# Attention with four PSUM banks for the scores, q and its transposition in one bank, and two heads' transposed probabilities per copy

## The chip, the cores and the metric

The kernel runs on one core of one Trainium2 chip. The metric is the device time of one execution in microseconds, as the median of several runs. The same inputs and outputs hold for both versions. Eight PSUM banks of 512 fp32 elements per partition are available to a core; TensorE writes into them, VectorE and ScalarE read them.

## The reference, cut to what matters

A layer of attention (one key and value head for 16 query heads of 64, cosine scores with a relative position bias, a causal mask and a null key), a layer norm, and a feed-forward part with fake quantisation, added to x. x is (8, 256, 128).

```python
xn = ln(x, g_norm)
q = (xn @ Wq).reshape(b, n, HEADS, DIM_HEAD).transpose(0, 2, 1, 3)
kv = xn @ Wkv
k, v = (kv[..., :DIM_HEAD], kv[..., DIM_HEAD:])
...
q = l2norm(q) * q_scale
k = l2norm(k) * k_scale
sim = jnp.einsum('bhid,bjd->bhij', q, k) * SCALE
...
attn = jax.nn.softmax(sim, axis=-1)
out = jnp.einsum('bhij,bjd->bhid', attn, v)
out = out.transpose(0, 2, 1, 3).reshape(b, n, HEADS * DIM_HEAD)
return ln(out @ Wout, g_out)
...
x = x + ffn(attention(x))
```

## The kernel before, in words

Each engine has its own instruction stream, written out by hand; semaphores tie them together. The attention is a loop over groups (`over_groups`, L91): 8 batches of 4 groups of 4 heads, and two groups more to drain. The functions named `group` at L418 (GpSimd), L540 (ScalarE), L812 (TensorE) and L1172 (VectorE) each set their own engine's order. What belongs to one group of heads runs over three groups of the loop: scores and exponentials in its own, turning (transposing) the probabilities in the next (`turned`), the value product and the output product in the one after (`summed`).

For a pair of heads TensorE makes the scores (`scores`, L764) in banks 0 and 1, one head per bank, 258 columns for the second block of rows and 129 for the first. VectorE adds the bias and takes the row maximum (`score_pair`, L1113). ScalarE takes the exponential and the row sum (`exponent`, L516). VectorE inverts the row sums of a pair (`invert`), and GpSimd multiplies the probabilities by them (`normalise`, L410). TensorE turns each head's three 128-blocks (`turn`, L799) into bank 2 or 3, and ScalarE copies them into `pT`, 384 columns per head (`pT_evac`, L526). The value product (`values`, L783) goes into bank 4, VectorE copies it out (`oT_copy`), and `y_products` (L736) multiplies it by Wout into bank 7, over the four groups of a batch. `null_weights` (L730) and `y_null` add the null key's part.

In between, q of the next quarter batch (128 rows, 8 heads) is made: product (`q_make`, L638) into bank 5, square on ScalarE (`q_square`, L476), row sums on VectorE (`q_norm2`), power -0.5 on GpSimd (`q_power`, L380), scaling on VectorE (`q_normalise`, L981), transposition on TensorE (`qT_make`, L652) into bank 6, copy on VectorE (`qT_evac`, L988). Once per batch the same happens for x (normalised rows `xn`, `x_power` L372, transposed), for k and v (`kv_make`, `k_power`, `k_normalise` L971 which makes `kz`, `kT_make`), and for the layer norm of the output (`y_stats`, `y_power`, `y_normalise` L1138, `yT_make`). Their small transpositions share bank 6 with q's: at each group's end TensorE waits until VectorE has copied q out (`qT_ready`) and then makes the small one.

A score pair waits until VectorE has read the pair before it (`scored`), since both use banks 0 and 1:

```python
if g > 0:
    pe.wait_ge(scored, 2 * g)
```

Of the kernel before, what the change touches and what calls it, by code (L numbers as in the profile page):

```python
# [33 lines left out]
P = 128  # L34
# [24 lines left out]
class Group:  # L59


    def __init__(self, at):
        self.at = at
        self.b, self.g = at // GB, at % GB
        self.par = self.b % 2
# [8 lines left out]
        self.made = c + 1 if 4 <= c + 1 < GB * B else None  # L74

# [21 lines left out]
def build(nc, x, cond, mask, g_norm, Wq, Wkv, q_scale, k_scale, null_bias, w0, b0, g0, w1, b1, g1, w2, b2,  # L97
# [3 lines left out]
    with ExitStack() as ctx:  # L101
# [122 lines left out]
        bank = [ctx.enter_context(nc.psum_tensor(f"bank{i}", [P, 512], F32)) for i in range(8)]  # L224
        score_ps, trans_ps = bank[0:2], bank[2:4]
        val_ps, q_ps, qT_ps, misc = bank[4], bank[5], bank[6], bank[7]
# [4 lines left out]

        null_out = qT_ps[0:H, N:2 * N]
# [119 lines left out]
        def _(pool):  # L352
# [55 lines left out]
            q_power(3, 3)  # L408

# [8 lines left out]
            def group(s):  # L418
                if s.quarter is not None and s.quarter >= 4:
                    q_power(s.quarter, s.quarter % 4)  # L420
                if s.g == 2 and s.prev is not None:
                    y_power(s.prev)
                if 1 <= s.at < GB * B:
                    normalise(heads(s.at - 1)[2:4])
                if s.at == GB * B:
                    normalise(heads(s.at - 1)[2:3])
                if s.g == 2 and s.next is not None:
                    k_power(s.next)
                if s.live:
                    normalise(heads(s.at)[0:2])  # L430
                if s.g == 1 and s.b + 2 < B:
                    x_power(s.b + 2)
# [17 lines left out]
        def _(act):  # L450
# [4 lines left out]
            def xT_evac(n, par, ps):  # L455
                act.wait_ge(xT_done, n + 1)
                act.copy(xTh[par][:, :], ps[:, 0:N]).then_inc(xT_ready, 1)
                act.copy(xTr[:, :], ps[:, 0:N][:, ::-1]).then_inc(xT_ready, 1)

            def kv_evac(n, ps):  # L460
                act.wait_ge(kv_done, n + 1)
                act.copy(kv[:, :, :], ps[:, 0:N].rearrange("p (t c) -> p t c", t=2)).then_inc(kv_ready, 1)

            def v_copy(n, par):
# [4 lines left out]
                act.copy(val[par][:, :, :], kv[:, :, D:2 * D]).then_inc(v_ready, 1)  # L469

            def kT_evac(n, par, ps):
                act.wait_ge(kT_done, n + 1)
                act.copy(kT[par][:, :].rearrange("p (b k) -> p b k", b=2)[:, :, 1:P + 1],
                         ps[:, 0:N].rearrange("p (b k) -> p b k", b=2)).then_inc(kT_ready, 1)
# [25 lines left out]
            kv_evac(0, misc)  # L500
# [8 lines left out]
            kT_evac(0, 0, misc)  # L509
            v_copy(0, 0)  # L510
# [833 lines left out]
```

## Time and profile before

| | |
|---|---|
| median of 3 runs | 310.94 us (310.54 to 310.96) |
| the profiled execution | 309.61 us |
| its span, first to last instruction | 307.8 us |
| mean granted TensorE clock | 0.975 of full |
| TensorE matmul busy | 262.3 us (85%) |
| TensorE weight loads busy | 207.9 us (68%) |
| VectorE busy | 242.8 us (79%) |
| ScalarE busy | 224.9 us (73%) |
| GpSimd busy | 206.6 us (67%) |

Busy times are of the whole span. The attention loop takes the span from 26 to 271 us; before it lie loads and the position table, behind it the feed-forward part. PE is TensorE, PEld its weight loads, DVE VectorE, ACT ScalarE, POOL GpSimd. A matmul's end in the profile is modelled: the next one of the same stream starts before it, so spacing is read from starts.

### The profile page before, as it was taken

The page shows a single profiled execution, that of the slowest core. Times are in us where ns is not written, and L with a number is a line of the kernel's source. Part 1 is how long each engine was busy: PE and PEld are TensorE (multiplying, and loading weights), DVE is VectorE, ACT ScalarE, POOL GpSimd, SP SyncE. Part 2 cuts the span into 40 slices and gives each one's busy share as a digit, 9 for nine tenths or more (in the row PEclk, how much of TensorE's full clock was granted, in tenths as well). Part 3 has the DMA queues.
Part 4 walks back from the last instruction along what each step waited for, and adds up shares of the span by engine and source line. Part 5 has one row for each costly group of instructions (what it writes and reads, how often), then busy time and mean ns, then how long its engine had stood idle before and what let it go on. Part 6 is the DMA issues. An engine that isn't in the chain of part 4 may idle for free.

```text
span 307.8 us, 7322 instructions
## 1 busy us (share of the span) xinstructions
PE 262.3 (85%) x2176; PEld 207.9 (68%) x2176; DVE 242.8 (79%) x976; ACT 224.9 (73%) x771; POOL 206.6 (67%) x393
## 2 busy tenths in 40 slices
PE   0767699999899989999998999899999998876251
PEld 0326578888688868877886888688878877561040
DVE  2978658788878888887888788868787876659985
ACT  1265678897889788978897888878888887437661
POOL 2786677679777877788789778887888755211401
PEclk9999699999999999999999999999999999999958
DMA  6369000000000000000000000000000020000005
GB/s 144 64 163 254 3 1 2 1 2 1 2 1 2 1 4 2 0 2 2 2 0 3 2 2 0 2 1 3 2 1 3 1 72 1 2 0 0 0 2 142
DMA packets 13084, 6.89 MB, mean 22 GB/s; under 512 B 1954, under 2 KB 12914, under 8 KB 13043
## 3 DMA queue, kind: packets, MB, share of 16 engines
q1 hardware_dynamic: 12466, 6.13, 8.0%
q8 instruction: 20, 0.33, 0.5%
q10 hardware_dynamic: 576, 0.26, 0.4%
q14 instruction: 22, 0.17, 0.2%
HBM read 5.31 MB, written 1.07 MB: 21 GB/s over the span
## 4 chain that ended last, share of the span: by engine, by line
PE 50%; DVE 21%; POOL 14%; issue 7%; ACT 5%; DMA 1%; ACTq 0%; POOLq 0%; DVEq 0%
PE bank L777 13%; PE bank L809 10%; PE bank L794 9%; PE bank L747 6%; POOL prob L415 5%; DVE score L1119 4%; PE bank L642 4%; POOL rq L370 3%; PE bank L658 3%; ACT prob L522 2%; DVE hmax L1252 2%; DVE kz L968 2%; DVE oT L1289 2%; DMA g0b<-in_L_cond_g_dram 1%; POOL rstd L370 1%
## 5 line engine op out<-in xcount | busy, mean ns | idle before, releaser
L522 ACT ACTIVATE prob<-score,negmax 128x258 f32<-128x258 f32 (+1 forms) x256 | 114.8, 454 | 30.3 <-DVE negmax L1119 30.1
L415 POOL TENSOR_SCALAR prob<-prob,rrow 128x258 f32<-128x258 f32 x254 | 109.2, 447 | 40.7 <-DVE rrow L1127 37.5
L1119 DVE CUSTOM_DVE_ANT_0 score<-bank,bias 128x258 f32<-128x258 f32 (+1 forms) x256 | 76.6, 355 | 20.9 <-PE bank L777 20.8
L532 ACT COPY pT<-bank 128x384 f32<-128x384 f32 x128 | 58.1, 480 | 15.3 <-PE bank L809 15.3
L777 PE MATMUL bank<-kT,qT 64*128 64x258 f32 (+1 forms) x512 | 60.1, 354 | 4.4 <-DVE negmax L1119 4.0
L777 PEld LDWEIGHTS bank<-kT,qT 64*128 64x128 f32 x512 | 44.6, 188 | 20.1 <-DVE negmax L1119 11.8
L809 PE MATMUL bank<-ident,prob 128*128 128x128 f32 x384 | 55.3, 280 | 1.0 <-ACT pT L532 1.0
L370 POOL TENSOR_TENSOR rq<-qn,neghalf 128x8 f32<-128x8 f32 x32 | 54.1, 1691 | 2.7
L809 PEld LDWEIGHTS bank<-ident,prob 128*128 128x128 f32 x384 | 43.7, 143 | 10.0 <-issue 1.7
L794 PE MATMUL bank<-pT,val 128*64 128x256 f32 (+1 forms) x512 | 48.7, 332 | 1.0 <-ACT pT L532 0.8
L522 ACT ACTIVATION_READ_ACCUMULATOR prob<-score,negmax 128x1 f32 x256 | 49.4, 193 | 0.0
L794 PEld LDWEIGHTS bank<-pT,val 128*64 128x64 f32 x512 | 31.7, 136 | 14.5 <-ACT pT L532 1.6
L747 PE MATMUL bank<-wout,oT 128*128 128x128 f32 x256 | 33.9, 275 | 0.8 <-DVE oT L1110 0.8
L747 PEld LDWEIGHTS bank<-wout,oT 128*128 128x128 f32 x256 | 31.1, 192 | 1.0 <-DVE oT L1110 1.0
L979 DVE TENSOR_REDUCE qn<-sq 128x8 f32<-128x512 f32 x32 | 21.6, 676 | 6.7 <-ACT sq L479 6.6
L1110 DVE COPY oT<-bank 128x512 f32<-128x512 f32 x32 | 21.8, 682 | 2.4 <-PE bank L794 2.4
L1127 DVE RECIPROCAL rrow<-rowsum 128x4 f32<-128x4 f32 x64 | 11.1, 174 | 14.5 <-ACT prob L522 14.5
L985 DVE TENSOR_TENSOR qn<-bank,rq 128x512 f32<-128x512 f32 x32 | 21.9, 685 | 0.6 <-POOL rq L370 0.3
L990 DVE COPY qT<-bank 128x512 f32<-128x512 f32 x32 | 21.5, 673 | 0.8 <-PE bank L658 0.8
L1119 DVE DVE_READ_ACCUMULATOR2_ANT negmax<- 128x1 f32 x256 | 21.2, 83 | 0.0
L658 PE MATMUL bank<-ident,qn 128*128 128x128 f32 x128 | 19.8, 278 | 0.7 <-DVE qn L985 0.7
L479 ACT ACTIVATE sq<-bank 128x512 f32<-128x512 f32 x32 | 18.8, 587 | 2.0 <-DVE qn L979 0.8
(161 smaller groups left out, 340.2 us busy)
## 6 DMA issues: line engine op xcount, KB each, us to landing
bias<-relative_table SPq DMA_DIRECT2D x8, 256.0 KB, 5.3
out_dram<-prob SPq DMA_DIRECT2D x4, 256.0 KB, 3.0
X<-in_x_dram SPq DMA_DIRECT2D x1, 896.0 KB, 12.1
prob<-in_L_cond_Wq_dram SPq DMA_DIRECT2D x1, 512.0 KB, 5.5
wout<-in_L_cond_Wout_dram SPq DMA_DIRECT2D x1, 512.0 KB, 13.3
prob<-in_L_ffn_w_down_dram SPq DMA_DIRECT2D x1, 176.0 KB, 2.4
X<-in_x_dram SPq DMA_DIRECT2D x1, 128.0 KB, 4.1
prob<-in_L_ffn_w_gate_dram SPq DMA_DIRECT2D x1, 128.0 KB, 2.0
```

Source lines behind the costliest of these rows:

```text
L370: pool.tensor_tensor(dst, src, neghalf[:, 0:width], ALU.pow).then_inc(done, 1)
L415: pool.tensor_scalar(prob[:, par, h, cols], prob[:, par, h, cols], rrow[:, par, h, t:t + 1], 1.0, ALU.mult, ALU.mult).then_inc(normed, 1)
L522: act.activation(prob[:, par, h, cols], score[:, h % 4, cols], ACT.Exp, scale=-1.0, bias=negmax[:, par, h, t:t + 1], accum_out=rowsum[:, p ...
L532: act.copy(pT[:, h % 4, :], trans_ps[h % 2][:, 0:3 * P]).then_inc(pT_ready, 1)
L658: last = pe.transpose(qT_ps[:, k * P:k * P + P], head_pair, ident[:, :])
L747: pe.matmul(y_out(t), oT[:, m % 2, k, t * P:t * P + P], wout[:, k, :], start=k + t == 0, stop=False, skip_group_check=True)
L777: product = pe.matmul(score_ps[a][:, at:at + KEYS1 - c0], qT[par][rows, h // 2, t * P:t * P + P], kT[par][rows, c0:KEYS1], start=not maske ...
L794: last = pe.matmul(val_ps[a * D:a * D + D, pair * N + i0:pair * N + N], val[m % 2][:, blk, :], pT[:, 2 * pair + a, c0:c1], start=blk == 1, ...
L809: last = pe.transpose(trans_ps[h % 2][:, k * P:k * P + P], prob[:, par, h, c0:c0 + P], ident[:, :])
L985: dve.tensor_tensor(qn[:, :, :], ps[:, :].rearrange("p (h d) -> p h d", d=D), rq[:, q, :].unsqueeze(2).broadcast_to([P, 8, D]), ALU.mult). ...
L1110: dve.tensor_copy(oT[:, m % 2, 2 * g:2 * g + 2, :].rearrange("p k n -> p (k n)"), val_ps[:, :])\
L1119: dve.tensor_tensor_reduce(score[:, h % 4, c0:c0 + w], ps[:, c0:c0 + w], bias[:, h, 0:w], -1.0, -3.0 * NEG, ALU.add, ALU.min, negmax[:, pa ...
```

## The change

PSUM is divided anew. `front` holds four score banks (0 to 3), two per pair of heads; `trans` (banks 4 and 5) receives the turned probabilities, and its second bank, bank 5, is also the value product's; q and its transposition share bank 6; bank 7 stays. The last 128 columns of both `trans` banks (`tails`) take the small transpositions and the null weights.

- `scores` uses the banks of its pair and waits for the scores of a whole group before. The value product comes first in a group, then both score pairs.
- `pT_evac` copies two heads, 768 columns, with one instruction; `values` waits for both copies.
- ScalarE's order is: q's square, exponentials of heads 2 and 3 of the group before, head 0, first copy, the small evacuation, head 1, second copy, null weights.
- TensorE interleaves the small transpositions with the first two turns; the next two turns wait for their evacuation (`low_out`). q's transposition stands between two halves of the output products, the q product at the group's end, behind q's copy.
- VectorE's and GpSimd's orders follow; yT is scaled by ScalarE, wql is made by GpSimd.

```diff
-        score_ps, trans_ps = bank[0:2], bank[2:4]
-        val_ps, q_ps, qT_ps, misc = bank[4], bank[5], bank[6], bank[7]
+        front = [psum(f"front{i}", 2) for i in range(2)]
+        trans = psum("trans", 2)
+        bank = [pair[:, i, :] for pair in (*front, trans) for i in range(2)]
+        bank += [psum(f"bank{i}", 1)[:, 0, :] for i in range(6, 8)]
+        score_ps, trans_ps = bank[0:4], bank[4:6]
+        val_ps, q_ps, misc = bank[5], bank[6], bank[7]
+        tails = trans[:, :, 3 * P:4 * P]
...
-            def pT_evac(at, i):
-
-                g, _, h = heads(at)[i]
-                act.wait_ge(pT_done, g + 1)
+            def pT_evac(at, pair):
+
+                g, _, h = heads(at)[2 * pair]
+                act.wait_ge(pT_done, g + 2)
                 if at > 0:
                     act.wait_ge(o_done, at)
-                act.copy(pT[:, h % 4, :], trans_ps[h % 2][:, 0:3 * P]).then_inc(pT_ready, 1)
+                ps = front[pair] if at == GB * B - 1 else trans
+                act.copy(pT[:, 2 * pair:2 * pair + 2, :], ps[:, :, 0:3 * P]).then_inc(pT_ready, 1)
...
+                if s.quarter is not None and s.quarter >= 4:
+                    q_square(s.quarter, q_ps)
+                if s.turned is not None:
+                    exponent(heads(s.turned)[2])
+                    exponent(heads(s.turned)[3])
                 if s.live:
                     exponent(heads(s.at)[0])
...
+                if s.turned is not None:
+                    pT_evac(s.turned, 0)
...
-                if g > 0:
-                    pe.wait_ge(scored, 2 * g)
+                banks = score_ps[2 * pair:2 * pair + 2]
+                if g >= GH:
+                    pe.wait_ge(scored, 2 * (g - 2))
...
-                pe.wait_ge(pT_ready, GH * (at + 1))
+                pe.wait_ge(pT_ready, 2 * (at + 1))
...
+                elif g > 1 and g % 2 == 0:
+                    pe.wait_ge(pT_ready, g // 2)
+                if i == 1 and s.summed is not None:
+                    pe.wait_ge(oT_ready, s.summed + 1)
+                if i < 2:
+                    low_make(s, i)
+                if i == 2:
+                    low_out(s)
+                if i >= 2 and s.null is not None and not last:
+                    if i == 2:
+                        pe.wait_ge(normed, 2 * g + 4)
+                    null_weights(s.null, i - 2)
...
+                if s.summed is not None:
+                    if s.g == 1 and s.prev is not None:
+                        pe.wait_ge(n_ready, s.prev + 1)
+                    values(s.summed)
...
                 if s.made is not None:
+                    pe.wait_ge(qT_ready, s.made)
```

How the order moves is seen at two places.

TensorE around a value product, in the loop's early groups, before (banks 0 and 1 scores, 2 and 3 turns, 4 values, 7 output):

```order
L747 MATMUL bank7<-wout,oT 128x128 [waits oT_ready]
L747 MATMUL bank7<-wout,oT 128x128 x3
L754 MATMUL bank7<-unull,pnT 128x128 [waits n_ready]
L754 MATMUL bank7<-unull,pnT 128x128
L628 MATMUL bank6<-wkv,xTr 128x128 [waits xT_ready,qT_ready]
L628 MATMUL bank6<-wkv,xTr 128x128
L777 MATMUL bank0<-kT1,qT1 128x258 [waits scored,qT_ready]
L777 MATMUL bank1<-kT1,qT1 128x258
L777 MATMUL bank0<-kT1,qT1 128x129
L777 MATMUL bank1<-kT1,qT1 128x129
L794 MATMUL bank4<-pT,val1 64x256 [waits oT_ready,v_ready,pT_ready]
L794 MATMUL bank4<-pT,val1 64x256
```

The same engine now, from q's transposition to the next value product:

```order
L696 MATMUL bank6<-ident,qn 128x128 [waits qT_ready,q_norm]
L696 MATMUL bank6<-ident,qn 128x128 x3
L792 MATMUL bank7<-wout,oT 128x128 x2
L888 MATMUL trans<-ident,prob 128x128 [waits xT_ready,pT_ready,normed]
L888 MATMUL trans<-ident,prob 128x128 x2
L888 MATMUL trans<-ident,prob 128x128 [waits normed]
L888 MATMUL trans<-ident,prob 128x128 x2
L680 MATMUL bank6<-wqh,xTh0 128x512 [waits q_norm,qT_ready]
L680 MATMUL bank6<-wql,xTh0 128x512
L680 MATMUL bank6<-wqh,xTl0 128x512
L835 MATMUL trans<-pT,val1 64x256 [waits oT_ready,pT_ready]
L835 MATMUL trans<-pT,val1 64x256
```

Before, the output products, the small ones and a score pair stood between the last turn and the value product; now it is the q product alone, and the value product writes the bank that was turned into.

VectorE in a batch's third group, before (from the row sums of k squared; yn is the normalised output, oT the copied value product):

```order
L962 ISA ksq,kn2<-kv 128x64 [waits kv_ready]
L962 ISA kn2 128x1
L962 ISA ksq,kn2<-kv 128x64
L962 ISA kn2 128x1
L985 TENSOR_TENSOR qn<-bank5,rq 128x512 [waits qT_done,q_rq]
L1142 TENSOR_SCALAR yn<-bank7,omv,ors 128x128 [waits y_rstd]
L1142 TENSOR_SCALAR yn<-bank7,omv,ors 128x128
L1110 COPY oT<-bank4 128x512 [waits o_done]
L1119 ISA score,negmax<-bank0,bias 128x258 [waits s_done]
L1119 ISA negmax 128x1
L1119 ISA score,negmax<-bank0,bias 128x129
```

And now:

```order
L1202 TENSOR_SCALAR yn<-bank7,omv,ors 128x128 [waits y_rstd]
L1202 TENSOR_SCALAR yn<-bank7,omv,ors 128x128
L1179 ISA score,negmax<-front0,bias 128x258 [waits s_done]
L1179 ISA negmax 128x1
L1179 ISA score,negmax<-front0,bias 128x129
L1179 ISA negmax 128x1
L1179 ISA score,negmax<-front0,bias 128x258 [waits s_done]
L1179 ISA negmax 128x1
L1179 ISA score,negmax<-front0,bias 128x129
L1179 ISA negmax 128x1
L1046 TENSOR_TENSOR qn<-bank6,rq 128x512 [waits qT_done,q_rq]
```

The scaling of q (`qn<-bank,rq`) stood behind both heads of a pair and right ahead of yn; now yn is ahead of the first scores, and they ahead of q's scaling.

## Rows read from the trace of the kernel before

**Rows 1.** Windows: us, each engine's busy us (xcount), PEclk, DMA share, GB/s

```profile
33.05:39.90 6.85, 5.38 (x23) 4.58 (x24) 5.08 (x26) 3.79 (x15) 4.04 (x9) 0.50 0.00 0
...
117.40:147.40 30.00, 28.92 (x256) 23.88 (x252) 24.61 (x109) 24.75 (x90) 24.12 (x47) 1.00 0.01 2
...
207.30:236.20 28.90, 28.89 (x256) 23.89 (x254) 23.79 (x105) 24.65 (x90) 23.09 (x45) 1.00 0.01 3
236.20:256.10 19.90, 19.42 (x175) 15.64 (x173) 14.88 (x72) 16.40 (x62) 14.24 (x31) 1.00 0.10 28
```

**Rows 2.** Order of time, TensorE, one batch: start us, us, what [idle before]

```profile
139.26 0.44 PE L635 MATMUL bank<-ident,kz 128*128 128x128 f32 x2 [1.08 <-DVE qT L990]
...
140.48 1.52 PE L794 MATMUL bank<-pT,val 128*64 128x256 f32 x16
142.00 0.93 PE L777 MATMUL bank<-kT,qT 64*128 64x258 f32 x8
142.86 0.88 PE L809 MATMUL bank<-ident,prob 128*128 128x128 f32 x6
...
143.93 0.47 PE L642 MATMUL bank<-wqh,xTh 128*128 128x512 f32 x1
...
144.70 0.82 PE L809 MATMUL bank<-ident,prob 128*128 128x128 f32 x6
145.35 1.06 PE L747 MATMUL bank<-wout,oT 128*128 128x128 f32 x8
```

**Rows 3.** Order of time, ScalarE, the same stretch

```profile
141.21 0.51 ACT L522 ACTIVATE prob<-score,negmax 128x258 f32<-128x258 f32 x1 [1.10 <-DVE negmax L1119]
...
142.10 0.50 ACT L522 ACTIVATE prob<-score,negmax 128x258 f32<-128x258 f32 x1
...
143.44 0.86 ACT L532 COPY pT<-bank 128x384 f32<-128x384 f32 x2 [0.37 <-PE bank L809]
```

**Rows 4.** Lines by form: busy us, mean ns, idle before; ScalarE's copies out of PSUM

```profile
L532 ACT COPY pT<-bank 128x384 f32<-128x384 f32 x128 | 58.1, 480 | 15.3 <-PE bank L809 15.3
...
L462 ACT COPY kv<-bank 128x256 f32<-128x256 f32 x8 | 3.0, 374 | 3.1 <-PE bank L628 2.8
```

**Rows 5.** Order of time, the last groups: a copy and the value product behind it

```profile
262.38 0.47 ACT L532 COPY pT<-bank 128x384 f32<-128x384 f32 x1
...
262.90 1.52 PE L794 MATMUL bank<-pT,val 128*64 128x256 f32 x16 [0.77 <-ACT pT L532]
```

**Rows 6.** Order of time, VectorE

```profile
126.33 0.68 DVE L985 TENSOR_TENSOR qn<-bank,rq 128x512 f32<-128x512 f32 x1
...
127.53 0.41 DVE L1119 CUSTOM_DVE_ANT_0 score<-bank,bias 128x258 f32<-128x258 f32 x1
...
128.64 0.17 DVE L1127 RECIPROCAL rrow<-rowsum 128x4 f32<-128x4 f32 x1
...
140.74 0.43 DVE L1119 CUSTOM_DVE_ANT_0 score<-bank,bias 128x258 f32<-128x258 f32 x1 [0.86 <-PE bank L777]
```

**Rows 7.** Lines by form: VectorE's products for kz

```profile
L968 DVE SCALAR_TENSOR_TENSOR kz<-kv,rk,qks 128x128 f32<-128x128 f32 x16 | 6.0, 414 | 1.7 <-POOL rk L370 1.7
```

**Rows 8.** Order of time, GpSimd

```profile
131.81 0.25 POOL L368 TENSOR_SCALAR qn<-qn 128x8 f32<-128x8 f32 x1
...
133.89 0.19 POOL L366 TENSOR_SCALAR omv<-omv 128x2 f32<-128x2 f32 x1
...
134.96 1.66 POOL L415 TENSOR_SCALAR prob<-prob,rrow 128x258 f32<-128x258 f32 x4
136.70 0.23 POOL L368 TENSOR_SCALAR kn<-kn 128x2 f32<-128x2 f32 x1
```

**Rows 9.** Start: GpSimd's first normalisation, its widest product, group four's value product

```profile
30.97 4.48 POOL L415 TENSOR_SCALAR prob<-prob,rrow 128x258 f32<-128x258 f32 x8 [2.44 <-DVE rrow L1127]
...
L443 POOL TENSOR_TENSOR prob<-prob 128x512 f32<-128x512 f32 x4 | 5.1, 1268 | 12.3 <-ACT prob L608 12.3
...
57.38 1.52 PE L794 MATMUL bank<-pT,val 128*64 128x256 f32 x16
```

More of the change, by code:

```diff
@@ L74, in __init__ @@
         self.made = c + 1 if 4 <= c + 1 < GB * B else None
+        self.turned = at - 1 if 1 <= at <= GB * B else None
+        self.summed = at - 2 if at >= 2 else None
+        late = 1 if self.first else 0
+        self.kv = self.next if self.g == late else None
+        self.kT = self.next if self.g == 1 + late else None
+        self.xT = self.b + 2 if self.g == 2 + late and self.b + 2 < B else None
+        self.yT = self.prev if self.g == 3 else None
+        self.null = self.prev if self.g == 0 else None
 def heads(at):
@@ L571, in group @@
+                if s.g == 1 and s.next is not None:
+                    v_copy(s.next)
                 if s.first and s.g == 1:
@@ L674, in _ @@
             pe.wait_ge(consts, 3)
-            xT_make(0, misc)
+            for t in range(2):
+                xT_make(0, t, halves(misc))
             mlp_turn(0)
@@ L681, in _ @@
             pe.wait_ge(wkv_ready, 1)
-            kv_make(0, misc)
+            for t in range(2):
+                kv_make(0, t, halves(misc))
             pe.wait_ge(wq_ready, 1)
@@ L691, in _ @@
             pe.wait_ge(kv_ready, 1)
-            kT_make(0, misc)
+            pe.wait_ge(kz_ready, 1)
+            pe.transpose(misc[:, 2 * P:3 * P], kz[:, 2, :], ident[:, :])
+            for t in range(2):
+                kT_make(0, t, halves(misc))
             q_make_first(2)
@@ L888, in ffn @@
             def ffn():
-                yT_make(B - 1)
+                for t in range(2):
+                    yT_make(B - 1, t)
                 keep_busy(8, q_ps)
@@ L1178, in group @@
+                if s.summed is not None:
+                    oT_copy(s.summed)
+                if s.kT is not None:
+                    k_normalise(s.kT)
+                if s.turned is not None:
+                    invert(heads(s.turned)[2:4])
+                if s.turned == GB * B - 1:
+                    last_normalise()
+                if s.g == 2 and s.prev is not None:
+                    y_normalise(s.prev)
                 if s.live:
+                    if s.first:
+                        dve.wait_ge(ld_bias[s.g], 16 * 2)
@@ L1197, in group @@
+                if s.g == 0 and s.prev is not None and s.b + 2 < B:
+                    x_normalise(s.b + 2)
+                if s.g == 3 and s.b + 3 < B:
+                    x_stats(s.b + 3)
+                if s.b == B - 1 and s.g == 2:
+                    ffn_weights(0)
                 if s.b == B - 1 and s.g == 3:
```

374 lines of the change are left out of this document (177 added, 197 removed).

## The prediction

> **What bounds the kernel now.** I read the windows first, to see how much of the time repeats, then TensorE's order of time inside one repeat, then the same stretch on ScalarE, VectorE and GpSimd. A batch is four groups of four heads and takes 30.0 us. TensorE is busy for 28.92 of them, VectorE for 24.61, ScalarE for 24.75 and GpSimd for 24.12, and TensorE's clock is full [rows 1]. So TensorE is nearly the bound, with two gaps. Before kz's transposition it idles 1.08 us, once per batch. And the second score pair starts exactly when the value product ends (140.48 plus 1.52 is 142.00), whereas the turns after it start 0.07 before its end [rows 2]; weight loads waited there for VectorE to empty the two score banks. I put that at 0.1 us, four times. Without both gaps a batch of TensorE work is 30.0 - 1.1 - 0.4 = 28.5 us. I split it by starts [rows 2]: value product 1.4 (its 1.52 less the gap), score pair 0.86, six turns (two heads) 0.71 and 0.65, transposition of q 0.36, q 0.77, output products 0.89 (1.06 less the 0.17 by which what follows overlaps, as 0.82 does before 145.35).
>
> **What goes.** Four score banks take away both gaps: score pairs never wait, and kz is no longer tied to q's copy. That is 1.5 us of each batch.
>
> **What the new order adds.** I walk one group of the new order, with 0 at the start of its value product. TensorE without any wait: first scores 1.4, second 2.25, turns of heads 0 and 1 with the small transposition between them to 4.05, half of the output products, q's transposition at 4.5, other half, turns of heads 2 and 3 at 5.3, q at 5.95, next value product at 6.7.
>
> *The wait for the copies.* The value product needs both copies of pT, and the banks of the turns are also its own, so only q's 0.77 us lies between the last turn and it. A copy starts 0.58 after the first turn of a pair of heads, of which three turns are the first head (142.86 to 143.44, [rows 2, 3]); there the pair of copies follows an idle moment, so I count 0.53 from the last head's first turn. The trace has no copy of 768 elements. From 256 elements (374 ns) to 384 (480 ns) an element costs 0.83 ns and the fixed part is 0.16 us [rows 4]. Two separate copies, 0.96 us, bound it above, 768 elements without a fixed part, 0.64, below; I take 0.16 + 0.64 = 0.80, since the two rows are of this very kind of copy. A value product starts 0.05 after the copy before it ends (262.38 + 0.47 to 262.90, [rows 5]). So last turn to value product takes 0.53 + 0.80 + 0.05 = 1.38, where the turns and q cover 1.1: **0.28 us lost in each group**, 1.1 per batch. In a batch's first group ScalarE also copies the null weights before the next value product may start: 0.25 more. ScalarE saves some 0.15 us per pair of copies, which nobody waits for.
>
> *The wait for the small evacuation.* Heads 2 and 3 turn only when the first copy (4.26 to 5.06) and the small one behind it are out: 0.37 for kv or kz, two for x, about 0.45 for y, then 0.05 to 0.1. That is 5.5 with y, where 5.3 was free: 0.2 lost. With x it is 6.0, but that group is later for another reason.
>
> *The wait for q's transposition.* VectorE copies the value product at 1.57 (0.05 behind its end), each such instruction 0.6 from start to start [rows 6]. ScalarE squares q from 0 on (512 elements, 0.59 by the slope of [rows 4], the last 0.1 of it under what follows), then does two heads of exponentials at 0.89 each [rows 3], so the row sums come at 2.35; scores are read 1.1 after their product starts (140.48 less 0.86, to 140.74 [rows 2, 6]), so at 2.5, and a pair takes 1.11 [rows 6]. Then q is scaled, 3.6 to 4.3, in time for 4.5. But the second group of a batch has kz's two instructions (414 ns each, [rows 7]) ahead of the scores, and the third has the two of yn, of the same size: scaled q comes at 4.8 and 5.0, so q's transposition at 4.9 and 5.06, not 4.5. **0.3 and 0.55 us lost.**
>
> *GpSimd.* One power of q is 2.08, of the small ones 1.07 and a normalisation of two heads 1.74 [rows 8]. Heads 0 and 1 end only 1.2 into the next group. In a batch's first group x's power follows, then q's: rq at 4.3 instead of 3.5, q's transposition at 5.1 where 4.75 (with kv's products) was free, and the normalised heads 2 and 3 at 6.05, which the null weights' transposition waits for together: **0.6 us lost**.
>
> Added up, from value product to value product: 8.3 in a batch's first group, 7.8 (with the null product) in its second, 7.7 in its third, 7.2 in its fourth, **31.1 us per batch against 30.0**. The gaps that go are worth 1.5, those that come 2.6.
>
> **The sum.** Batches 1 to 5: 5 x 1.1 = +5.5. Batch 6 has no x work and takes 28.9 now [rows 1]; the same walk without x's power gives 30.4: +1.5. Batch 7's first three groups take 19.9 [rows 1]; without q and kz the copies are even less covered: 7.5, 7.1 and 7.2, +1.9, and +0.6 in the fourth group and behind it, where two heads' exponentials move behind the last score pair. yT's scaling goes from VectorE to ScalarE at the same 0.4 to 0.5 us; the activation table load now stands behind it, with 2 us to spare.
> The start gains. GpSimd is free at 28.5 (30.97 less 2.44 of idleness). It gets wql: not in the trace there; its bounds are 1.3, the 512-element product, and twice that, 2.5; I take 2.5, since wql has 1,024 elements [rows 9]. Heads 0 and 1 are then normalised by 32.8, the first copy waits for ScalarE until 34.4, heads 2 and 3 turn at 35.6, q at 36.3, the null product follows, and the first value product starts at 39.0. Two groups of 7.4 lead to 53.8, where it is 57.4 now [rows 9]: -3.6. TensorE's clock stood at 0.50 from 33.05 to 39.90 [rows 1], behind its idle stretch; TensorE still waits for GpSimd there after the change, so I expect it to fall again and give back 1.1: **-2.5**. With no fall it would be -3.6 or better.
> *By the Trainium skill, "TensorE: Matmul & The Clock Gate", Part 1, the halved clock is the idle state and sustained work releases it; the idle stretch gets shorter, so by that rule the sum would be 1.1 lower.*
>
> Sum: -2.5 + 5.5 + 1.5 + 1.9 + 0.6 = +7.0 on the profiled execution's 309.6, that is 316.6. The median of the runs is 310.9, 0.4% above that execution; I forecast **317**.
>
> **Rivals.**
> *A, not slower: only the copies' wait comes.* If the powers and VectorE's order run ahead of TensorE by half a microsecond more than in my walk, the losses for q's transposition and the small evacuation vanish, and the batch is 28.5 + 1.1 + 0.25 = 29.9. It decides at the point where scaled q comes before 4.5 in the second and third group. Then batches 1 to 5 give -0.5, batch 6 +0.9, batch 7 +2 and the start -3.6: 308. For it: VectorE and GpSimd are idle 5.4 and 5.9 us per batch now [rows 1]. Against it: the order on VectorE is fixed, and kz's and yn's work stands between.
> *B, faster: all the gaps were buffers.* TensorE falls to 28.5 per batch: 6 x -1.5, nothing in batch 7, -3.6 at the start: 297. Against it: the copies' wait has nothing over it but q.
> *By the Trainium skill, "Perfetto Trace Analysis", Identifying Performance Opportunities, a gap that repeats on the engine that should be saturated can mean too few buffers in PSUM. The trace agrees for TensorE's two gaps; that rule is B.*
> *C, more slower: the losses chain.* From q's transposition through its copy, the fourth head's score, the reciprocal, the normalisation, a power, q's power and its scaling runs a ring of 0.65 + 0.58 + 0.56 + 0.4 + 1.74 + 2.1 + 0.7, about 6.7, and 1.07 more with each of the three small powers: 30.0 per batch by itself. A wait of TensorE that falls into this ring lengthens it. At 32 per batch: 309.6 + 10 + 3 + 2.5 - 2.5 = 322.
> That the change does not do what it says is excluded for the instructions: each group of the new order has two copies of 768 elements and four bank names for scores.
>
> **The numbers.** The walk as it stands has 0.62, C 0.16, A 0.13 (ending on both sides of no change: 0.10 faster, 0.03 same), B 0.06, another cause of no change 0.03. A measurement can tell about 0.2%, 0.6 us. Faster 0.16, same 0.06, slower 0.78. The range: the copy's bounds are 32 groups times 0.16 us either way, 5 us, and half of that where other waits cover it; wql and the clock 1.5; a tenth missed in each group 3. These together give some 5 to 6 either way. That is 311 to 323 for the walk; to leave out no more than 2 in 10 it reaches to A, **306 to 323**.
>
> **What would show it.** Right: TensorE waiting for ScalarE's pT before the value products in every group; copies near 800 ns; batches of 31 us, the third group no longer the longest; q's transposition waiting for VectorE's qn in the second and third groups; no score product waiting for negmax; the value product of group four near 54 to 55. Wrong: batches under 30 us, or copies much off 0.8.

## The result, and the profile after

The changed kernel takes 317.01 us (median of 5 runs, 316.79 to 319.11) where the kernel before took 310.94 in the same session (5 runs, 310.54 to 312.32): ratio 1.021, 95% interval 1.017 to 1.026. It is 6.1 us slower. The profiled execution was the slowest of the five: 319.11 us, span 317.3. One execution of this study (of e8, 322.7 us) was in a slower state of the chip, and e8's median leaves it out.

Busy times of the page after, and two windows: from the first score product to the value product of group four, and one batch.

```profile
PE 262.3 (83%) x2175; PEld 205.0 (65%) x2176; DVE 242.5 (76%) x967; ACT 223.6 (70%) x715; POOL 207.5 (65%) x394
```

```profile
28.65:55.73 27.08, 25.08 (x212) 20.10 (x211) 21.79 (x104) 20.54 (x74) 19.60 (x36) 1.00 0.07 15
117.67:148.73 31.06, 29.00 (x253) 23.46 (x253) 25.08 (x109) 24.54 (x84) 23.74 (x47) 1.00 0.01 2
```

The work of a batch is what it was, TensorE 29.00 us against 28.92 [rows 1], and the clock is full. But the batch is 31.06 long, not 30.0. TensorE is now 2.06 us short of its batch's length, where it was 1.08 short. The waits of after, for whole runs (us in total, times, longest), say where:

```profile
PEld trans L835 <- ACT pT L559: 15.9, 23, 1.1
...
PEld bank L696 <- DVE qn L1046: 11.9, 21, 1.9
...
PEld trans L835 <- ACT pnT L563: 7.3, 8, 1.2
PE trans L835 <- ACT pT L559: 6.5, 23, 0.9
...
PE bank L696 <- DVE qn L1046: 6.2, 13, 0.9
```

Score products (L818) wait for no negmax any more; that wait, and kz's, are what the change removes. In the kernel before they were:

```profile
PEld bank L777 <- DVE negmax L1119: 11.8, 33, 3.1
...
PEld bank L635 <- DVE qT L990: 6.6, 6, 1.3
```

In their place the value product (L835) waits for ScalarE's copies, and q's transposition (L696) for VectorE's scaled q. In order of time, TensorE, the first three groups of a batch:

```profile
148.73 1.52 PE L835 MATMUL trans<-pT,val 128*64 128x256 f32 x16 [0.19 <-ACT pT L559]
...
153.94 0.66 PE L696 MATMUL bank<-ident,qn 128*128 128x128 f32 x4 [0.43 <-DVE qn L1046]
...
157.23 1.52 PE L835 MATMUL trans<-pT,val 128*64 128x256 f32 x16 [0.44 <-ACT pnT L563]
...
161.85 0.66 PE L696 MATMUL bank<-ident,qn 128*128 128x128 f32 x4
...
164.95 1.52 PE L835 MATMUL trans<-pT,val 128*64 128x256 f32 x16 [0.19 <-ACT pT L559]
...
169.94 0.66 PE L696 MATMUL bank<-ident,qn 128*128 128x128 f32 x4 [0.48 <-DVE qn L1046]
...
172.63 1.52 PE L835 MATMUL trans<-pT,val 128*64 128x256 f32 x16 [0.19 <-ACT pT L559]
```

From value product to value product the four groups take 8.50, 7.72, 7.68 and (172.63 to 179.79) 7.16 us. The group with kz, the longest before (8.25), is no longer the longest; the first one is, with both waits in it. And the copy of two heads, with VectorE's products for kz (a pair):

```profile
L559 ACT COPY pT<-trans 128x768 f32<-128x768 f32 x62 | 49.2, 793 | 18.4 <-PE trans L888 16.8
```

```profile
159.41 0.60 DVE L1029 SCALAR_TENSOR_TENSOR kz<-kv,rk,qks 128x128 f32<-128x128 f32 x2
```

Two spans say all that follows in few numbers: the **start**, from the first score product to the first value product, and the **loop**, from the first value product to the last (32 of them). The start begins between 25.7 and 29.0 us in the 14 profiles of this study, in no order that follows an edit. In the profile of after it began 2.74 later than in the one of before. The chain that ended last has a load (of k's scale) in it there, and TensorE's clock was at half from 21.3 to 28.3 us:

```profile
24.00:28.65 4.65, 4.65 (x19) 3.33 (x18) 2.84 (x6) 1.53 (x2) 3.92 (x6) 0.54 1.13 306
```

Such a fall ahead of the first scores is in the profiles of after, e2 and e6 only, and each of these three executions is 1.3 to 2.2 us above the median of its kernel (e5's, with no fall, is 1.5 above). The kernel before had none in its profile. Behind the last value product VectorE's last instruction starts 36.2 later in before and 36.0 later in after:

```profile
303.67 0.69 DVE L1314 TENSOR_TENSOR prob<-prob,X 128x512 f32<-128x512 f32 x1
```

```profile
311.94 0.69 DVE L1366 TENSOR_TENSOR prob<-prob,X 128x512 f32<-128x512 f32 x1
```

The first is of before, the second of after. From its end to the end of the span, where only the last store is left, before has 3.4 us and after 4.7. That too is not the change's: it is 3.4 or 3.6 in two profiles (before, and e8, which is made from after) and 4.6 to 4.9 in the other twelve, four of them made from before.

| | start | loop | behind | ahead |
|---|---|---|---|---|
| before | 17.72 | 223.87 | 40.3 | 25.91 |
| after | 12.41 | 234.86 | 41.4 | 28.65 |
| difference | -5.31 | +10.99 | +1.1 | +2.74 |

The first two are the change's: +5.7 us, close to the +6.1 of the medians. The last two are not, and complete the 9.5 by which the two profiled spans differ.

### The profile page after: what moved, and what is told of

It reads as the page before. It is cut to its first block, busy times and chain, and to the rows that moved or that the text cites. A ratio compares the mean times of both kernels' runs of the same rounds, so it can differ in the third digit from the quotient of the medians.

```text
span 317.3 us, 7164 instructions
## 1 busy us (share of the span) xinstructions
PE 262.3 (83%) x2175; PEld 205.0 (65%) x2176; DVE 242.5 (76%) x967; ACT 223.6 (70%) x715; POOL 207.5 (65%) x394
## 3 DMA queue, kind: packets, MB, share of 16 engines
HBM read 5.31 MB, written 1.07 MB: 20 GB/s over the span
## 4 chain that ended last, share of the span: by engine, by line
PE 41%; DVE 24%; ACT 12%; issue 9%; POOL 8%; DMA 4%; SPq 1%; POOLq 0%; ACTq 0%; DVEq 0%
PE trans L835 10%; PE trans L888 8%; PE bank L696 6%; PE front L818 5%; PE bank L792 5%; DVE score L1179 5%; ACT prob L548 4%; DVE qn L1046 4%; ACT pT L559 4%; DMA ks<-in_L_cond_k_scale_dram 4%; POOL rq L388 3%; DVE oT L1170 2%; DVE hmax L1304 2%; POOL prob L435 2%; DVE yn L1202 2%
## 5 line engine op out<-in xcount | busy, mean ns | idle before, releaser
L1179 DVE CUSTOM_DVE_ANT_0 score<-front,bias 128x258 f32<-128x258 f32 (+1 forms) x256 | 77.9, 352 | 3.1 <-PE front L818 2.9
L559 ACT COPY pT<-trans 128x768 f32<-128x768 f32 x62 | 49.2, 793 | 18.4 <-PE trans L888 16.8
L835 PE MATMUL trans<-pT,val 128*64 128x256 f32 (+1 forms) x512 | 48.7, 332 | 10.5 <-ACT pT L559 6.5
L888 PE MATMUL trans<-ident,prob 128*128 128x128 f32 x372 | 55.5, 274 | 1.9 <-ACT kv L484 1.0
L835 PEld LDWEIGHTS trans<-pT,val 128*64 128x64 f32 x512 | 31.7, 136 | 32.7 <-ACT pT L559 15.9
L818 PE MATMUL front<-kT,qT 64*128 64x258 f32 (+1 forms) x512 | 51.1, 338 | 0.0
L818 PEld LDWEIGHTS front<-kT,qT 64*128 64x128 f32 x512 | 41.7, 187 | 8.7 <-issue 5.6
L888 PEld LDWEIGHTS trans<-ident,prob 128*128 128x128 f32 x372 | 42.8, 141 | 3.6 <-issue 1.4
L1170 DVE COPY oT<-trans 128x512 f32<-128x512 f32 x32 | 22.1, 692 | 13.2 <-PE trans L835 12.9
L696 PE MATMUL bank<-ident,qn 128*128 128x128 f32 x128 | 21.7, 294 | 7.1 <-DVE qn L1046 6.2
L696 PEld LDWEIGHTS bank<-ident,qn 128*128 128x128 f32 x128 | 14.3, 146 | 12.7 <-DVE qn L1046 11.9
## 6 DMA issues: line engine op xcount, KB each, us to landing
X<-in_x_dram SPq DMA_DIRECT2D x1, 896.0 KB, 12.4
```

Of the source, the lines that this page charges most:

```text
L559: act.copy(pT[:, 2 * pair:2 * pair + 2, :], ps[:, :, 0:3 * P]).then_inc(pT_ready, 1)
L696: last = pe.transpose(q_ps[:, k * P:k * P + P], head_pair, ident[:, :])
L818: product = pe.matmul(banks[a][:, at:at + KEYS1 - c0], qT[par][rows, h // 2, t * P:t * P + P], kT[par][rows, c0:KEYS1], start=not masked, ...
L835: last = pe.matmul(val_ps[a * D:a * D + D, pair * N + i0:pair * N + N], val[m % 2][:, blk, :], pT[:, 2 * pair + a, c0:c1], start=blk == 1, ...
L888: product = pe.transpose(ps[:, k * P:k * P + P], prob[:, par, h, c0:c0 + P], ident[:, :])
L1170: dve.tensor_copy(oT[:, m % 2, 2 * g:2 * g + 2, :].rearrange("p k n -> p (k n)"), val_ps[:, :])\
```

## The experiments

Twelve kernels ran, each against the kernel before. The names e and b say from which kernel one was made, after or before. Groups are the distances between value products in a batch in the middle of the loop. Ratios are to the kernel before in the same session; its own median lay between 310.4 and 311.8 there, so differences of the medians of two sessions are good to a microsecond or so, and start and loop say more.

| | median us | ratio to before | start | loop | first, second, third, fourth group |
|---|---|---|---|---|---|
| before | 310.9 | | 17.72 | 223.87 | 7.16, 7.61, 8.25, 6.93 |
| after | 317.0 | 1.021 (1.017 to 1.026) | 12.41 | 234.86 | 8.50, 7.72, 7.68, 7.16 |
| e1 | 320.3 | 1.032 (1.027 to 1.038) | 12.50 | 238.26 | 8.50, 7.72, 8.12, 7.15 |
| e2 | 314.1 | 1.011 (1.006 to 1.016) | 12.41 | 232.02 | 7.87, 7.71, 7.68, 7.15 |
| e3 | 312.7 | 1.006 (1.003 to 1.009) | 12.50 | 230.53 | 8.40, 7.66, 7.56, 6.94 |
| e4 | 312.2 | 1.005 (1.002 to 1.009) | 12.41 | 230.07 | 8.46, 7.65, 7.62, 6.81 |
| e5 | 312.0 | 1.002 (1.000 to 1.005) | 12.40 | 229.89 | 7.37, 7.82, 8.12, 6.90 |
| e6 | 308.8 | 0.992 (0.988 to 0.996) | 12.42 | 226.17 | 7.55, 7.66, 7.55, 6.95 |
| e7 | 308.0 | 0.989 (0.984 to 0.994) | 12.39 | 225.76 | 7.36, 7.83, 7.62, 6.81 |
| e8 | 317.7 | 1.023 (1.016 to 1.030) | 13.54 | 234.88 | 8.50, 7.71, 7.68, 7.16 |
| b1 | 308.3 | 0.992 (0.989 to 0.996) | 18.05 | 221.24 | 7.72, 7.62, 7.17, 6.94 |
| b2 | 307.4 | 0.989 (0.984 to 0.994) | 14.16 | 223.95 | 7.15, 7.62, 8.26, 6.93 |
| b3 | 305.1 | 0.983 (0.977 to 0.988) | 14.16 | 221.19 | 7.71, 7.61, 7.17, 6.93 |
| b4 | 302.0 | 0.971 (0.966 to 0.976) | 14.16 | 218.47 | 7.15, 7.62, 7.17, 6.94 |

**e1: yn behind q's scaling.** Is q's transposition late in the third group because the two instructions of yn stand ahead of it on VectorE? They move behind it; since the output products write the bank that yn reads, q's transposition moves ahead of them in this group.

```diff
-                if s.g == 2 and s.prev is not None:
-                    y_normalise(s.prev)
                 if s.live:
...
                     q_normalise(s.quarter, s.quarter % 4, q_ps)
+                if s.g == 2 and s.prev is not None:
+                    y_normalise(s.prev)
...
+                if s.g == 2 and s.quarter is not None:
+                    qT_make(s.quarter)
                 if s.summed is not None:
                     y_products(s.summed, 0)
-                if s.quarter is not None:
+                if s.g != 2 and s.quarter is not None:
                     qT_make(s.quarter)
```

> The changed kernel; in each batch's third group q's scaling stands ahead of yn on VectorE, and q's transposition ahead of the first output products on TensorE. Theory (the walk): q's transposition then starts near 4.4 us after the value product instead of 5.0, but heads 2 and 3 still wait for x's evacuation, which ends at about 5.9 either way, so the third group goes from 7.68 to 7.5 to 7.7 and the whole by 0 to -1.2 us. Rival (q's transposition alone sets that group): it falls by 0.5 us in each batch, -3 us or more in all. Under the rival of chained losses it would be more, since the ring through q gets shorter.

Measured 320.3, and the loop is 3.4 us longer than after's: a miss. Order of time in e1, VectorE first, then GpSimd, then TensorE, of the third group, whose value product starts at 163.78:

```profile
167.75 0.69 DVE L1048 TENSOR_TENSOR qn<-bank,rq 128x512 f32<-128x512 f32 x1 [0.18 <-POOL rq L388]
```

```profile
164.92 0.71 POOL L388 TENSOR_TENSOR ors<-omv,neghalf 128x2 f32<-128x2 f32 x1
165.72 0.25 POOL L386 TENSOR_SCALAR qn<-qn 128x8 f32<-128x8 f32 x1
166.05 1.67 POOL L388 TENSOR_TENSOR rq<-qn,neghalf 128x8 f32<-128x8 f32 x1
```

```profile
168.50 0.66 PE L696 MATMUL bank<-ident,qn 128*128 128x128 f32 x4 [0.66 <-DVE qn L1048]
169.22 1.13 PE L792 MATMUL bank<-wout,oT 128*128 128x128 f32 x8
```

VectorE now waits for GpSimd's rq, which comes 3.94 behind the value product, since y's power stands ahead of q's there too. In after, q's scaling starts at 4.24 (169.19), so yn was worth only 0.27 us (4.99 to 4.72 for the transposition). TensorE, with the output products now behind it, stands idle 0.66 where it was idle 0.48 with half of them done. So the wait has two causes within 0.3 us of each other. That the longer group comes from the output products, which no longer cover the wait, fits these rows; e1 moved both things at once, so the two were not told apart.

**e2: x's power off q's path.** In after it is the last of the fourth group on GpSimd and so ahead of q's power of the next batch's first group. It moves behind that group's first normalisation.

```diff
                 if s.at == 1:
                     x_power(2)
+                if s.g == 0 and s.b > 0 and s.b + 2 < B:
+                    x_power(s.b + 2)
                 if s.live:
                     normalise(heads(s.at)[0:2])
-                if s.g == 3 and s.b + 3 < B:
-                    x_power(s.b + 3)
```

> The changed kernel; x's power moves on GpSimd from the end of a batch's fourth group to behind q's power and heads 2 and 3 in the next batch's first group, where GpSimd is idle for 1.25 us. Theory: q's scaling no longer waits in the first group and the null weights' transposition finds both heads normalised; the first group goes from 8.50 to about 7.8 in batches 1 to 5, -3.5 us in all. Rival (the null weights' copy behind the second copy sets that group, or the wait moves into the second group, which then has x's power ahead of k's): less than -1 us.

Measured: 2.9 us off, all of it in first groups: 0.63 (8.50 to 7.87) in batches 2 to 4, 0.45 and 0.47 in batches 1 and 5. That is the 0.6 which the prediction gave to GpSimd in this group.

**e3 and e4: the size of the copies.** In e3 heads 2 and 3 are copied by one instruction each, so the copy of head 2 runs while head 3 is turned. In e4 all four heads have their own copy, with the small evacuation between the first two.

```diff
+                ps = front[pair] if at == GB * B - 1 else trans
+                if pair == 1:
+                    for a in range(2):
+                        act.wait_ge(pT_done, g + a + 1)
+                        act.copy(pT[:, 2 + a, :], ps[:, a, 0:3 * P]).then_inc(pT_ready, 1)
+                    return
                 act.wait_ge(pT_done, g + 2)
...
-                pe.wait_ge(pT_ready, 2 * (at + 1))
+                pe.wait_ge(pT_ready, 3 * (at + 1))
...
```

> The changed kernel; heads 2 and 3 of pT are copied by one instruction each, the first while the last head still turns; heads 0 and 1 stay with one instruction. Theory (only q's product covers the second copy): the value product starts 0.3 us earlier in each of some 32 groups, by 0.35 or so where no q product follows, -8 to -10 us in all, so about 308. Rival 1 (the ring through q and GpSimd of 30.0 us per batch holds): at most -1 us per batch, -6 to -7, and the wait reappears before q's transposition. Rival 2 (the copy is long whatever its form, or ScalarE is the bound): 0 to -2 us.

> As e3_split, and heads 0 and 1 are also copied by one instruction each, the small evacuation between them, so the turn of head 2 waits for one copy of 384 and the small evacuation. Theory: beyond e3_split the first turn of head 2 comes 0.3 us earlier where an evacuation of x or y delays it (third and fourth group): -0.3 to -0.5 us per batch, -2 to -3 us beyond e3_split, about 306. Rival: q's transposition holds these groups anyway, and the result is that of e3_split within 0.5 us.

Measured -4.3 and -4.8 us (medians, and the same in the loop). TensorE in e3, same three groups:

```profile
150.94 0.66 PE L701 MATMUL bank<-ident,qn 128*128 128x128 f32 x4 [0.64 <-DVE qn L1051]
...
153.92 1.52 PE L840 MATMUL trans<-pT,val 128*64 128x256 f32 x16
...
158.75 0.66 PE L701 MATMUL bank<-ident,qn 128*128 128x128 f32 x4 [0.31 <-DVE qn L1051]
...
161.58 1.52 PE L840 MATMUL trans<-pT,val 128*64 128x256 f32 x16
...
166.63 0.66 PE L701 MATMUL bank<-ident,qn 128*128 128x128 f32 x4 [0.54 <-DVE qn L1051]
...
169.14 1.52 PE L840 MATMUL trans<-pT,val 128*64 128x256 f32 x16
```

No idle time of TensorE stands before these value products any more. In the fourth group, which waits for nothing else, that gives 0.22 (e4: 0.35). In the first three the idle time before q's transposition grows, from 0.43 to 0.64, from 0 to 0.31 and from 0.48 to 0.54, and they gain only 0.10, 0.06 and 0.12. So TensorE now catches up with the ring through q, the powers and the normalisations, as the rival of these runs said; the sum of single losses, 8 to 10 us, was wrong because one wait hides behind the other.

*The Trainium skill, "Perfetto Trace Analysis", Optimizing Scalar/DVE Operations, says that grouping pays where the engine is saturated, and that splitting instructions may let work finish sooner where ScalarE or VectorE is not saturated but causes gaps elsewhere. By that rule the copies of this change should not be joined; the trace agrees, with ScalarE busy 24.54 of 31.06 us and 4.3 us to gain by the split.*

**e5: three edits at once.** e1's, e2's and e4's.

> The changed kernel with e1, e2 and e4 together. Theory (the losses are separate and add up to what the four banks freed): -3.5 from x's power, -10 to -12 from the copies, -1 to -2 from q ahead of yn now that x's evacuation is earlier; 301 to 304, faster than the kernel before by over 2%, batches of 28.7 to 29 us. Rival (the ring through q's power binds next): 305 to 308, with TensorE waiting for qn in every group.

Measured 312.0, against 301 to 304 and 305 to 308 expected: both fell. The first group fell to 7.37, by 1.13, where e2 alone took 0.63 off it and e4 alone 0.04: each of the two waits had hidden behind the other. But the third group stood at 8.12, e1's value. Which of the three was guilty was open, hence the next two.

**e6 and e7: e2 with e3, e2 with e4.**

> Made from the changed kernel: x's power moved one group later, behind the first normalisation of the next batch's first group, and the copies of heads 2 and 3 made one by one. By themselves the two gave -2.9 and -4.3 us. Theory (each removes another wait, so they add): 317.0 - 7.2 = 309.8 us, first group of a batch 8.50 - 0.6 - 0.1 = 7.8 us. Rival (with the copies short, x's power is the one thing that the first group still waits for, as the run with three edits suggests, where that group takes 7.37): first group 7.4, the batch 29.7 to 29.9, 308 us or less.

> As the run before, with all four heads copied one by one; it is also the run with three edits without its edit to the scaling of y. Theory: the third group returns from 8.12 to 7.6 us and the fourth stays at 6.8 to 6.9, so the batch falls from 30.2 to 29.7, and the time from 312.0 to 309 us, or 307.5 by the loss of 0.9 us per batch against the run with the four copies alone. Rival (the third group's loss is not the scaling of y but x's power standing elsewhere on GpSimd): third group stays above 8.0 and the time near 312.

Measured 308.8 and 308.0. In e6 the first group is 7.55, between theory and rival, and the whole is 308.8, a microsecond under the theory. In e7 the third returns to 7.62, as its theory said: e1's edit was the harm in e5. So the new bank layout, with two edits, is 1.1% faster than the kernel before. The second group gets longer in e7 (7.83), again at q's transposition, 0.44 idle there, with the power of k ahead of q's. The batch of e7 (that of b4, to compare, stands below):

```profile
112.52:142.15 29.63, 28.42 (x254) 23.38 (x253) 25.05 (x109) 24.98 (x91) 23.63 (x47) 1.00 0.01 1
```

TensorE is idle 1.21 us of it; 0.44 and 0.54 of that stand before q's transposition in the second and third group.

**e8: one part undone.** wql is made by VectorE again, at the end of its first group.

```diff
-            pool.wait_ge(wq_high, 1)
-            pool.tensor_tensor(wql[:, :], wq[:, :], wqh[:, :].bitcast(F32), ALU.subtract).then_inc(wq_low, 1)
...
                     x_stats(2)
+                    dve.wait_ge(wq_high, 1)
+                    dve.tensor_tensor(wql[:, :], wq[:, :], wqh[:, :].bitcast(F32), ALU.subtract).then_inc(wq_low, 1)
```

> Made from the changed kernel, one part undone: wql is made by VectorE again, at the end of its first group. Theory (the start's gain lies almost all in this move: 1.42 us of VectorE in front of the second group's scores, and the fall of TensorE's clock that follows the longer wait): first score pair to value product of group four goes from 27.1 to 30.5 or 31, the granted clock falls to about 0.6 between 10 and 17 us behind the first scores, and the time is 3 to 4 us above 317.0. Rival (the clock keeps full because of the four score banks, not because of wql): +1.4 us and a clock of 1.00 throughout.

Measured 317.7, +0.7 on the medians, which cannot tell that from nothing, and +1.13 in the start; the clock stayed at 1.00 all through. The theory, half the clock and 3 to 4 us, fell; the rival was right about the clock, and its +1.4 is close to the start's +1.13. From the first scores to group four's value product:

```profile
26.96:55.18 28.22, 25.08 (x212) 20.15 (x212) 22.96 (x104) 20.56 (x74) 19.95 (x37) 1.00 0.18 42
```

**b1: x's power in the kernel before.** It stood at the end of the second group on GpSimd; it moves to the end of the fourth.

```diff
-                if s.g == 1 and s.b + 2 < B:
+                if s.g == 3 and s.b + 2 < B:
                     x_power(s.b + 2)
```

> The kernel before; x's power moves on GpSimd from the second group of a batch to its fourth. Theory: the stall of 1.1 us before kz's transposition came from the powers of x, q, y and k following each other on GpSimd; without x's in that row it goes or shrinks to 0.1, -1.0 us in each of batches 0 to 5, about -5 to -6 us (305). Rival (the stall is a buffer's: kz's transposition shares the bank with q's): it stays, 0 to -1 us.

Measured 308.3, where the kernel before had 311.2 in the same session, -2.9: less than expected. The third group lost its whole gap (8.25 to 7.17), so the 1.08 us ahead of kz's transposition came from this power. But the first group grew by 0.56; the same 1.07 us now queued ahead of its power of q, and b4 below takes the 0.56 away by moving it again.

**b2: only wql to GpSimd, in the kernel before.**

```diff
             q_power(3, 3)
+            pool.wait_ge(wq_high, 1)
+            pool.tensor_tensor(wql[:, :], wq[:, :], wqh[:, :].bitcast(F32), ALU.subtract).then_inc(wq_low, 1)
...
-                if s.first and s.g == 0:
-                    dve.wait_ge(wq_high, 1)
-                    dve.tensor_tensor(wql[:, :], wq[:, :], wqh[:, :].bitcast(F32), ALU.subtract).then_inc(wq_low, 1)
```

> The kernel before; wql is made by GpSimd behind q's fourth power, as in the changed kernel, instead of by VectorE (1.42 us ahead of the scores of group 1). Theory: the changed start gained 4.4 us (first score pair to value product of group 4 took 27.1 against 31.5 us) mainly by the four score banks and the new order, so this alone gives -1 to -2 us or nothing, since GpSimd's 2.5 us stand ahead of the first normalisation. Rival: it is the wql move that kept TensorE's clock at full there: -3 us or more.

Measured 307.4, -3.8; start -3.56, loop unchanged. First scores to group four's value product, of before and of b2:

```profile
25.91:57.38 31.47, 27.85 (x218) 22.97 (x218) 22.50 (x101) 22.76 (x86) 21.65 (x41) 0.89 0.18 42
```

```profile
26.93:54.84 27.91, 25.52 (x218) 20.95 (x218) 21.31 (x100) 22.55 (x86) 23.00 (x42) 1.00 0.14 33
```

Same instructions on TensorE, 2.33 us less busy time, and a clock of 1.00 instead of 0.89. So about 2.3 of the 3.56 us are the clock and 1.2 the place in VectorE's queue: an estimate, which takes all of the busy time saved as lying on the path. In e8, where the clock stays, 1.13 is all that there is.

**b3 and b4: the kernel before, improved.** b3 has both edits. b4 puts x's power of the fourth group ahead of its second normalisation, where GpSimd waited 0.96 us for the reciprocals.

```diff
+                if s.g == 3 and s.b + 2 < B:
+                    x_power(s.b + 2)
                 if s.live:
                     normalise(heads(s.at)[0:2])
-                if s.g == 3 and s.b + 2 < B:
-                    x_power(s.b + 2)
```

> The kernel before with both: the sum of the two, if they don't meet; about 304 to 305.

> Made from the kernel before with both edits that helped it (wql on GpSimd, x's power in the fourth group): x's power moves ahead of that group's second normalisation, into 0.96 us in which GpSimd waits for the reciprocals. Theory: q's power of the next batch's first group then no longer queues behind it, the first group falls from 7.71 to 7.16 us, and the batch from 29.44 to 28.9: 305.1 - 5 x 0.55 = 302.3 us. Rival (the normalisation behind it, now 0.1 to 0.2 later, delays the turns): no change against 305.1.

b3 gave 305.1, b4 302.0, each within half a microsecond of what was expected; b4 is 2.9% under the kernel before. A batch of b4:

```profile
111.74:140.59 28.85, 28.82 (x254) 23.85 (x252) 24.27 (x109) 24.66 (x90) 24.07 (x47) 1.00 0.01 2
```

TensorE is busy 28.82 of 28.85 us. With two pieces of work moved the old bank layout is at its bound, and 6 us faster than the best version of the new one that was tried. What four score banks have left to win in it is, by the walk, 0.1 us in each group, at the second score pair. No run isolates that, but the fourth group of e4 and e7, where no idle time of TensorE shows and the products are the same, takes 6.81 against 6.93 in b4.

## Why the prediction was right, and where it was off

The forecast was 317 and the time is 317.0. Its walk held in the middle of the loop and was off at both ends.

- **The batch.** Predicted 8.3, 7.8, 7.7, 7.2, measured 8.50, 7.72, 7.68, 7.16; 31.1 (its four terms add up to 31.0) and 31.06 together. Batch 6 was to take 30.4 and took 30.37, batch 7's first three groups 21.8 and 21.94. Batches 1 to 7's share, predicted +8.9 (5.5, 1.5 and 1.9), measured +8.68 (5.18, 1.51 and 1.99).
- **What goes.** Both gaps went, as forecast. For kz's the bank was not needed, though: the forecast tied it to q's copy, and b1 removed it in the old layout by moving a power on GpSimd.
- **The copies' wait.** 0.80 for 768 elements, measured 0.793; 0.28 lost per group, measured 0.19 of idle time in the rows and 0.22 in e3's fourth group. It is not to be had in full: e3 won 0.5 of the 1.1 per batch, and 0.7 and 0.9 in the last two, where less work stands in q's ring.
- **The small evacuation.** 0.2 was forecast in the fourth group. No idle time stands before the turns of heads 2 and 3 there, and e4, which takes it off the path, won 0.13 more than e3 in that group.
- **x's power in the first group.** 0.6 predicted, 0.63 by e2. The best supported term.
- **q's transposition in the third group.** The size was right, 0.55 predicted and 0.48 idle. The reason given, yn ahead of it on VectorE, was only half the matter: by e1 GpSimd's powers hold it to within 0.27 us of the same time. In the second group the step overstated: 0.3 predicted, none measured. It had taken kz's pair at 0.83, twice 414 ns [rows 7], and the pair took 0.60, since one instruction starts before the end of the one before it. That this group took 7.72 where 7.8 was forecast is a cancellation: only 0.19 of it shows as idle, so some 7.5 is work (an estimate), where the walk has 6.7 and 0.45 for the null product.
- **The start.** Mis-sized, in the helpful direction: -2.5 predicted, and from first scores to group four's value product 31.47 became 27.08, -4.4. Two steps failed. The clock was expected to fall again and did not: 1.00 in the window shown. Its price was too low as well: 1.1 was given back for it, where b2 shows 2.3 us of busy time. And without the fall the walk gave -3.6, 0.8 short; it started the first value product 13.1 behind the first scores, and it started 12.4 behind. Making wql on GpSimd took 2.44 us, as taken from the bounds (2.5); by b2 this move alone, with no bank added, is worth 3.56.
- **The last group and behind.** +0.6 predicted for the fourth group and what follows; the last two value products lie 12.77 behind the third group's where it was 11.38, +1.4. What the text had was two heads' exponentials; the trace also shows TensorE idle 0.92 before the last value product, for the null weights' copy, and 0.89 before the one ahead of it, for pT. The +1.1 behind the last value product is the end of the last store, and not of the change.

Together: +7.0 forecast; the start is 1.9 better, the last groups 0.8 worse, the batches 0.2 better, so +5.7 in the two spans of the profiles and +6.1 in the medians. That 317.0 was met to the tenth is luck: the sum, 316.6, was rounded up and made on an execution 1.3 under its median, and errors of 1.9 and 0.8 pulled against each other. What held is the batch: its mechanism, its sum, and most of its terms, but for the second group's 0.3 and the first group's 0.2 too little.

**The rivals.** A, only the copies' wait comes, was excluded by batches over 31 us. B, all gaps were buffers, likewise. Its half about kz's gap fell in b1 too: a power on GpSimd made that gap, and moving one line took it away with no bank added. *By the Trainium skill, "Perfetto Trace Analysis", Identifying Performance Opportunities, a repeating gap can mean too little PSUM; here the larger gap, 1.08 us per batch, did not.* C, the ring, was priced at 30.0 us per batch by itself and did not decide in after. The waits before q's transposition say that e3, e4 and e7 ran into it: with the copies split the batch stopped at 30.5, and at 29.6 once one of the three small powers no longer stood ahead of q's. No run changed the ring alone.

**What stays open.** How much of what e7 still loses against b4 (29.6 against 28.9 per batch) is y's and k's power on GpSimd, and how much VectorE's order, was not taken apart; the bank that yn reads and the output products write keeps the two from being exchanged simply.

## What to carry to other kernels

Before giving more banks to a gap, ask which instruction ends it: here the engine behind the wait (GpSimd, with one 1.07 us power in the wrong place) was cured by moving a line into an idle moment, and the kernel came to its TensorE bound in the old layout. A joined copy that saves its engine 0.17 us (793 ns against twice 480) lengthens the time from the last producer to the first reader, and that is a loss wherever the reader has nothing else to do; join only where the engine itself is the bound. Losses found one by one in a walk do not add when undone one by one: run the edits together, and leave each out once.

## What the runs showed that was not expected

- **TensorE's clock** fell behind the first scores in the kernel before (to 0.50, [rows 1]) and in b1 (to 0.50), and in no other kernel of this study. In both TensorE had just stood idle for VectorE's negmax, 2.86 and 2.87 us long, and the fall came within that stretch. In b2, b3 and b4 the same wait is 1.63 or 1.64 long, and there is no fall. From 31 to 34 us TensorE was busy 0.65 of 3 us in before, and 0.50 followed; in b2, which began 1.0 us later, it was 1.25 of 3, with 2.70 of 3 behind it:

```profile
31.00:34.00 3.00, 0.65 (x8) 0.41 (x6) 2.17 (x7) 1.60 (x7) 3.00 (x5) 0.84 0.05 8
34.00:37.00 3.00, 2.48 (x12) 2.08 (x13) 2.07 (x11) 1.59 (x8) 1.45 (x4) 0.50 0.00 0
```

```profile
31.00:34.00 3.00, 1.25 (x11) 0.77 (x9) 1.91 (x15) 2.83 (x12) 2.90 (x6) 1.00 0.04 8
34.00:37.00 3.00, 2.70 (x21) 2.36 (x22) 2.85 (x18) 2.64 (x13) 1.52 (x5) 1.00 0.00 0
```

  The first fence is of before, the second of b2. The lower level is 1.2 GHz and the full one 2.4. The same 1.42 us instruction on VectorE so cost 3.56 us in the one layout and 1.13 in the other. The idle stretch alone does not settle it, though: ahead of the first scores the clock fell in the profile of e2 after one of 1.66 us, and did not in before, e1, e7, b3 and b4 after ones of 1.67 to 1.70. One profile per kernel does not show how often it falls. *By the Trainium skill, "TensorE: Matmul & The Clock Gate", Part 1, the lower level is the idle state and work releases it; before agrees, where 1.00 returned at 40 us after TensorE had been busy 5.38 of 6.85 us at the lower level [rows 1].*
- **The end of a profile.** The last store's 1.2 us more or less, and the 3 us by which the first scores come earlier or later, belong to no edit; a microsecond between two single profiles says nothing about an edit until it is known to lie between the first score product and the last value product.
- **The copy from two banks** by one instruction (768 elements, 793 ns) costs what the slope between 256 and 384 elements in one bank gave, 0.80; there is no price for the second bank. *The Trainium skill, "ScalarE: Activation LUTs", What ACT_TABLE_LOAD costs, has 186 ns and 0.833 ns an element for an ACTIVATE with immediate scale and bias. For 768 elements that makes an estimate of 826 ns; the copy here, out of PSUM, took 33 ns less.*
